# Block 0's scores spread by VectorE and turned once in fp32; first up weights and block 1's normalisation on GpSimd

## The reference

```
x = x + attention(layernorm(x), ctx)         # q, k, v projections, softmax over 120 keys
h = layernorm(x)
probs = softmax(h @ router.T)                # 8 experts
k = argmax(clip(gelu(h @ w1.T + b1) @ w2.T + b2)) + 1        # 1 to 6, for each token
score[e] = probs[e] if rank(e) < k else 0
x = x + sum_e score[e] * (silu(h @ gate[e].T) * (h @ up[e].T)) @ down[e].T     # 336 hidden units each
```

## Time and profile before

| | |
|---|---|
| median of 3 runs | 754.36 us (754.0 to 754.42) |
| the profiled execution, its own time | 754.58 us |
| its span, first to last instruction | 752.8 us |
| granted TensorE clock | 1.000 |
| PE busy | 741.4 us (98%) |
| DVE busy | 646.3 us (86%) |
| POOL busy | 578.4 us (77%) |
| ACT busy | 550.5 us (73%) |

### The profile page before, as it was taken

The page is one execution under the profiler, slowest core; times in us unless marked ns, Lnnn a source line. Parts: engine busy times, 40 slices in busy tenths (PEclk is TensorE's granted clock), DMA queues, the critical chain, the costliest instruction groups (busy, mean ns, idle before and its releaser), DMA issues.

```text
span 752.8 us, 13834 instructions
## 1 busy us (share of the span) xinstructions
PE 741.4 (98%) x3721; PEld 364.5 (48%) x3721; DVE 646.3 (86%) x1395; ACT 550.5 (73%) x978; POOL 578.4 (77%) x620
## 2 busy tenths in 40 slices
PE   8999999999999999999999999999999999999998
PEld 5544454444545445454544545445454544444445
DVE  7999888898878889888898988889888897978877
ACT  5997777777777776777767777776877767777664
POOL 2687977879796886968689696886968688696864
PEclk9999999999999999999999999999999999999999
DMA  9200211304033142322323133142322312120110
GB/s 351 71 15 15 64 36 36 78 14 85 16 76 78 28 100 50 76 54 60 78 40 87 38 78 74 27 98 48 77 54 61 80 28 56 28 57 15 28 30 29
DMA packets 107272, 45.40 MB, mean 60 GB/s; under 512 B 86873, under 2 KB 97113, under 8 KB 107225
## 3 DMA queue, kind: packets, MB, share of 16 engines
q1 hardware_dynamic: 106792, 44.39, 24.6%
q10 hardware_dynamic: 432, 0.48, 0.2%
HBM read 26.46 MB, written 10.78 MB: 49 GB/s over the span
## 4 chain that ended last, share of the span: by engine, by line
PE 80%; issue 6%; POOL 5%; DVE 5%; ACT 2%; DMA 0%; POOLq 0%; DVEq 0%; SPq 0%; ACTq 0%
PE bank L631 24%; PE bank L633 24%; PE bank L632 24%; POOL weighted L1204 3%; DVE bank L1558 2%; PE bank L514 2%; PE bank L541 1%; PE bank L627 1%; DVE hid_lo L1564 1%; PE bank L525 1%; PE bank L590 1%; PE bank L768 1%; PE bank L609 1%; POOL v_early L1146 0%; POOL apart L1172 0%
## 5 line engine op out<-in xcount | busy, mean ns | idle before, releaser
L1204 POOL TENSOR_TENSOR weighted<-silu,score_bc 128x512 f32<-128x512 f32 x336 | 432.2, 1302 | 118.9 <-ACT silu L969 114.8
L963 ACT ACTIVATE hid_hi<-bank 128x512 f16<-128x512 f32 x336 | 200.7, 597 | 169.4 <-DVE bank L1558 166.0
L1558 DVE SCALAR_TENSOR_TENSOR bank<-bank,h_scale,weighted 128x512 f32<-128x512 f32 x336 | 252.8, 752 | 70.4 <-PE bank L633 39.8
L969 ACT ACTIVATE silu<-bank,silu_scale 128x512 f32<-128x512 f32 x336 | 230.7, 687 | 14.8 <-PE bank L633 14.2
L1564 DVE TENSOR_TENSOR hid_lo<-bank,hid_hi 128x512 f16<-128x512 f32 x336 | 227.8, 678 | 3.1 <-ACT hid_hi L963 2.3
L631 PE MATMUL bank<-xn_lo,up_hi 128*128 128x512 f16 x336 | 127.6, 380 | 2.6 <-DVE hid_lo L1564 2.4
L631 PE MATMUL bank<-xn_lo,gate_hi 128*128 128x512 f16 x336 | 127.6, 380 | 1.3 <-ACT silu L969 1.3
L633 PE MATMUL bank<-xn_hi,up_hi 128*128 128x512 f16 x336 | 127.4, 379 | 0.0
L632 PE MATMUL bank<-xn_hi,up_lo 128*128 128x512 f16 x336 | 127.4, 379 | 0.0
L633 PE MATMUL bank<-xn_hi,gate_hi 128*128 128x512 f16 x336 | 127.4, 379 | 0.0
L632 PE MATMUL bank<-xn_hi,gate_lo 128*128 128x512 f16 x336 | 127.4, 379 | 0.0
(11 more groups left out here) (200 smaller groups left out, 800.0 us busy)
## 6 DMA issues: line engine op xcount, KB each, us to landing
x_in<-in_x SPq DMA_DIRECT2D x16, 256.0 KB, 2.8
y_kept<-y_sb SPq DMA_DIRECT2D x60, 64.0 KB, 2.6
y_tok<-y_kept SPq DMA_DIRECT2D x15, 256.0 KB, 2.8
out<-out_sb SPq DMA_DIRECT2D x15, 256.0 KB, 2.2
xt_in<-in_x_t SPq DMA_DIRECT2D x14, 256.0 KB, 2.7
row_bc<-row_kept SPq DMA_DIRECT2D x14, 256.0 KB, 3.5
ctx_in<-in_ctx_t SPq DMA_DIRECT2D x14, 240.0 KB, 2.7
p_kept<-y_sb SPq DMA_DIRECT2D x10, 256.0 KB, 2.0
```

Source lines behind the costliest of these rows:

```text
L963: af(hid_hi[j % HRING][:], up_bank[j % U_BANKS][:], ACT.Copy).then_inc(hid_hi_ready, 1)
L969: af(silu[j % RING][:], gate_bank[(par + j) % G_BANKS][:], ACT.Silu, scale=silu_scale[:])\
L1204: g.tensor_tensor(weighted[j % RING][:], silu[j % RING][:], score_bc[par][:], ALU.mult)\
L1558: v.scalar_tensor_tensor(up_bank[j % U_BANKS][:], up_bank[j % U_BANKS][:], h_scale[:], weighted[j % RING][:], ALU.mult, ALU.mult).then_inc ...
```

## The change

Block 0's scores: VectorE's one `first_scores` writes the masked probability of each token 16 times side by side (128 tokens x 4 batches x 128 columns, fp32, into `y_tok`, which is free then); TensorE turns the four 128 x 128 pieces in fp32 straight into the bank that `score_spread` reads, which now also multiplies by 256. The split, the copy, the product with ones and zeros and their constants (one 64 KB DMA on ScalarE's queue) are gone. Further: the first third of up's high half, `weight_high(1)`, moves from ScalarE to GpSimd; `norm1` of block 1 moves from ScalarE to GpSimd as two operations over 128 x 512; block 1's values are copied out of PSUM by ScalarE, and GpSimd adds the bias in place (`value_bias(1)`). On TensorE `keys(5)` now stands ahead of `gate(0, 0, 2)` and of the score transposes. The counts of `v_raw_ready` go up by one, since one more value copy is counted.

```diff
-            def score_transposes(n):
-                pe.wait_ge(s16_ready, n + 1)
+            def score_transposes():
+                pe.wait_ge(score_ready, 1)
                 pe.wait_ge(below_ready, 2)
                 for b in range(BB):
-                    last = transpose(x0[0:2 * EXPERTS, :].bitcast(F16)[:, b * P:(b + 1) * P], score16[:, b, :],
-                                     ident16_sb)
-                last.then_inc(st_done, 1)
-
-            def score_broadcast(n):
-                pe.wait_ge(st_ready, n + 1)
-                mm(x0[:], sel_sb, score_t[:], start=True, stop=True).then_inc(bc_done, 1)
+                    last = transpose(x0[:, b * P:(b + 1) * P], y_tok[:, b * P:(b + 1) * P], ident_sb)
+                last.then_inc(bc_done, 1)
...
-            gate(0, 0, 2)
-            score_transposes(0)
             pe.wait_ge(kmin_ready, 1)
             keys(5, 1, x1)
-            score_broadcast(0)
+            gate(0, 0, 2)
+            score_transposes()
             attend(1, y_bank)
...
-            def norm1(n, par, lo, hi):
-                act.wait_ge(ln1_shift, n + 1)
-                wait(act, t1_done, n)
-                for b in range(lo, hi):
-                    last = af(xn_nat[:, b, :], x_in[par][:, b, :], ACT.Identity, bias=shift1[:, b:b + 1],
-                              scale=rstd1[par][:, b:b + 1])
-                if hi == BB:
-                    last.then_inc(xn_ready, 1)
...
-            def score_copy(n):
-                act.wait_ge(st_done, n + 1)
-                wait(act, bc_done, n)
-                af(score_t[:], x0[0:2 * EXPERTS, :].bitcast(F16)[:, 0:NT], ACT.Copy).then_inc(st_ready, 1)
-
             def score_spread(n, par):
                 act.wait_ge(bc_done, n + 1)
                 wait(act, weighted_ready, TILES * (n - 1))
-                af(score_bc[par][:], x0[:], ACT.Copy).then_inc(bc_ready, 1)
+                af(score_bc[par][:], x0[:], ACT.Copy, scale=S_SCALE).then_inc(bc_ready, 1)
...
-            norm1(1, 1, 0, 2)
             exps(0)
-            norm1(1, 1, 2, BB)
+            values(1, y_bank)
             turned_probs(0)
...
             exps(1)
-            weight_high(1)
             router_exps(0)
             nc.scalar.preload_act_table(ACT.Silu)
             gated(0, 0, 0)
             turned_probs(1, up_bank[1])
             weight_high(2)
-            score_copy(0)
+            score_spread(0, 0)
             gated(0, 0, 1)
-            score_spread(0, 0)
             weight_sums(8)
...
-                else:
+                elif n == 0:
                     g.tensor_tensor(shift1[:], less1[:], rstd1[par][:], ALU.mult).then_inc(ln1_shift, 1)
+
+            def norm1(n, par):
+                pool.wait_ge(ln1_less, n + 1)
+                pool.wait_ge(ln1_rstd, n + 1)
+                pool.wait_ge(t1_done, n)
+                g.tensor_tensor(xn_nat[:], x_in[par][:], over(less1[:], P), ALU.add).then_inc(ln1_shift, 1)
+                pool.wait_ge(ln1_shift, n + 1)
+                g.tensor_tensor(xn_nat[:], xn_nat[:], over(rstd1[par][:], P), ALU.mult).then_inc(xn_ready, 1)
...
             rstd_1(0, 0)
             rstd_1(1, 1)
+            norm1(1, 1)
             pool.wait_ge(rest_in, 16)
+            value_bias(1)
             rstd_2(0)
             weight_high(0, 0, FIRST_TILES)
             x2_low(0, 0)
             weight_high(0, FIRST_TILES, PART)
+            weight_high(1, 0, PART)
             route_probs(0)
             rank_over(0)
-            pool.wait_ge(s16_ready, 1)
+            pool.wait_ge(score_ready, 1)
             rstd_1(2, 0)
             weigh(0, 0, 0)
...
+            def first_scores():
+                dve.wait_ge(over_ready, 1)
+                shape = [P, BB, EXPERTS, ROWS]
+                v.scalar_tensor_tensor(y_tok[:].rearrange("p (b e r) -> p b e r", b=BB, e=EXPERTS),
+                                       rank_less[:].unsqueeze(3).broadcast_to(shape), 0.0,
+                                       prob[:].unsqueeze(3).broadcast_to(shape), ALU.is_le, ALU.mult)\
+                    .then_inc(score_ready, 1)
...
@@ -1698,9 +1676,7 @@
             route_rank(0)
             aggregate_1_waits(2)
             aggregate_1(2)
-            scores(0)
-            split_scores(0)
-            values(1, y_bank)
+            first_scores()
             weight_low(1)
```

More of the change, by code:

```diff
@@ L86, with program @@
 SKIPPED, LAST_LAG, FIRST_STILL = (10, 16), 5, 15
-def program(nc, x, x_t, ctx_t, consts, consts16, gate_t, up_t, down_t, out):
+def program(nc, x, x_t, ctx_t, consts, gate_t, up_t, down_t, out):
     x_blocks = x.rearrange("(t p) (b d) -> t p b d", b=BB, p=P)
@@ L209, in program @@
         out_sb = [sb(f"out_sb{k}", [P, BB, P]) for k in range(2)]
-        consts_in, rest_in, consts16_in = sem("consts_in"), sem("rest_in"), sem("consts16_in")
+        consts_in, rest_in = sem("consts_in"), sem("rest_in")
         weights_in = [sem(f"weights_in{n}") for n in range(9)]
@@ L246, in program @@
                              "score_ready"))
-        s16hi_ready, s16_ready, st_done, st_ready, bc_done, bc_ready = (
-            sem(n) for n in ("s16hi_ready", "s16_ready", "st_done", "st_ready", "bc_done", "bc_ready"))
+        bc_done, bc_ready = sem("bc_done"), sem("bc_ready")
         spread_hi_ready, score_up_ready, spread_lo_ready, units_in, rows_ready = (
@@ L600, in probs_transposes @@
                 if isinstance(n, int) and n == 1:
-                    pe.wait_ge(v_raw_ready, 2)
+                    pe.wait_ge(v_raw_ready, 3)
                 for b in range(BB):
@@ L621, in keys @@
                 if is_ahead(n):
-                    pe.wait_ge(v_raw_ready, 4)
+                    pe.wait_ge(v_raw_ready, 5)
                 elif dst is x1 and not is_early(n):
@@ L674, in up @@
                 if isinstance(t, int) and t == 0 and j == 2:
-                    pe.wait_ge(v_raw_ready, 3)
+                    pe.wait_ge(v_raw_ready, 4)
                 wait(pe, hid_lo_ready, n - U_BANKS + 1)
@@ L772, in _ @@
             pe.wait_ge(rest_in, 16)
-            pe.wait_ge(consts16_in, 16)
             turn_first_x()
@@ L796, in _ @@
             probs_transposes(1, up_bank[1])
-            pe.wait_ge(v_raw_ready, 1)
+            pe.wait_ge(v_raw_ready, 2)
             values(4, 0, up_bank[2])
             gate(0, 0, 1)
-            gate(0, 0, 2)
-            score_transposes(0)
             pe.wait_ge(kmin_ready, 1)
             keys(5, 1, x1)
-            score_broadcast(0)
+            gate(0, 0, 2)
+            score_transposes()
             attend(1, y_bank)
@@ L1035, in _ @@
             act.dma_start(consts_sb[:, FIRST_CONSTS:], consts[:, FIRST_CONSTS:]).then_inc(rest_in, 16)
-            act.dma_start(consts16_sb[:], consts16).then_inc(consts16_in, 16)
             act.wait_ge(consts_in, 16)
@@ L1144, in value_bias @@
             def value_bias(n):
-                pool.wait_ge(v_raw_ready, n - 1)
+                pool.wait_ge(v_raw_ready, n)
                 g.tensor_tensor(v_early[n][:].rearrange("p (b d) -> p b d", b=BB),
@@ L1415, in values @@
                 dve.wait_ge(vp_done, n + 1)
-                if not isinstance(n, int) or n != 1:
-                    wait(dve, o_done, n)
+                wait(dve, o_done, n)
                 v.tensor_tensor(values_of(n)[:].rearrange("p (b d) -> p b d", b=BB),
@@ L1420, in values @@
                                 bv_sb[0:CTX, :].unsqueeze(1).broadcast_to([CTX, BB, P]), ALU.add)\
-                    .then_inc(v_early_ready if isinstance(n, int) and n == 1 else v_ready, 1)
+                    .then_inc(v_ready, 1)
             def residual(n, par, lo, hi, src=x0):
@@ L1504, in route_rank @@
                 v.tensor_reduce(rank[:], ahead[:], AX.X, ALU.add).then_inc(rank_ready, 1)
+            def first_scores():
[5 more added lines that the diff above has]
+                    .then_inc(score_ready, 1)
             def scores(n):
                 dve.wait_ge(over_ready, n + 1)
-                if isinstance(n, int) and n == 1:
-                    dve.wait_ge(s16_ready, 1)
-                else:
-                    wait(dve, spread_lo_ready, n - 1)
+                wait(dve, spread_lo_ready, n - 1)
                 v.scalar_tensor_tensor(score[:], rank_less[:], 0.0, prob[:], ALU.is_le, ALU.mult)\
                     .then_inc(score_ready, 1)
-            def split_scores(n):
-                dve.wait_ge(score_ready, n + 1)
-                v.tensor_scalar(score16[:, :, 0:EXPERTS], score[:], S_SCALE, None, ALU.mult).then_inc(s16hi_ready, 1)
-                dve.wait_ge(s16hi_ready, n + 1)
-                v.scalar_tensor_tensor(score16[:, :, EXPERTS:], score[:], S_SCALE, score16[:, :, 0:EXPERTS], ALU.mult,
-                                       ALU.subtract).then_inc(s16_ready, 1)
             def result_squares(n):
@@ L1721 @@
     down = np.asarray(L0_ffn_down_w).reshape(EXPERTS, P, TILES, ROWS).transpose(0, 3, 2, 1).reshape(P, TILES * P)
-    col = np.arange(P)
```

(3 more changed lines are left out.)

5 lines of the change are left out of this document (removed).

## The result

The changed kernel takes 755.95 us in the median of 14 runs (755.22 to 756.39), the kernel before 754.35 in the median of 14 (754.0 to 754.99). The ratio is 1.0020, with a 95% interval from 1.0013 to 1.0027: 1.6 us slower, from 1.0 to 2.0. The profiled execution took 756.23 us, its span is 754.3.

What follows compares the result with a forecast made beforehand. TensorE, full from 130 to 220 us, was taken to keep any lead-in lateness: 754.58 us profiled plus 0.65 for the late first hidden product gives 755.2, less 0.2 for the median 755.0; range 754.3 to 755.7, with the first rival 753.5 to 755.9.

Steps and rivals of the forecast that it cites:

- The signs that it named: Profile after: `weight_low` near 2.3 us, first silu near 28.8, scores ready near 30.9, first weigh right behind `row`, `score_bc` long there.
- TensorE is full further on, and what is late stays: From 130 to 220 us TensorE is busy 90.00 of 90.00 us; its lateness on entering stays to the end.
- Up's high half holds gate's `weight_low`: Lead-in: GpSimd's operation, taken as 1.9 us, makes VectorE's 640-column `weight_low` get going 1.40 us later.
- ScalarE gives back 0.25: Router's exponentials, freed of up's high half, start 0.05 after VectorE's step instead of 0.30, leaving the chain 1.15 us late.
- `first_scores` 0.75: VectorE's new scores operation in the lead-in takes 0.75 us, between ends of 0.43 and 1.14; scores ready at 30.90.
- The short way is hidden behind `rstd_1(2, 0)`: Before the first weigh: 1.05 us gained for `score_bc`, but GpSimd runs `rstd_1(2, 0)` first; weigh starts 0.7 after `score_bc`.
- `rstd_1(2, 0)` takes 1.92 us as before: GpSimd ahead of the first weigh: runs from 30.98 to 32.90, so the weigh starts at 32.95, 0.84 late.
- Normalisation and the constants' load are worth nothing: Lead-in: block 1's normalisation fits GpSimd's idle 6.94 us up to 17.52; the 64 KB load is off every wait found.
- The two don't hold each other: Rival at gate's `weight_low`: no stall, first hidden product 0.7 early, 753.65 us; chance 0.17.
- the lateness is hidden: Rival: later waits of TensorE inside the first turn take the lateness in, 754.4 us; chance 0.14.
- One more meeting, 1.05 us, slower: Rival, first turn: a `weight_low` or `ahead` finds a weigh begun before it, costing 1.05 us, 756.1; chance 0.11.

Runs made afterwards that it cites:

- e_scores_only: Kernel before with only the short way of the scores and TensorE's order; 754.45 us against 754.42 for the kernel before.
- e_up_only: Kernel before with only up's first high half moved from ScalarE to GpSimd; 755.69 us against 754.73 for the kernel before.
- e_up_back: Changed kernel with up's first high half back on ScalarE; 755.22 us against 754.73 for the kernel before.
- e_gap: Changed kernel with block 1's values added by VectorE again, between `first_scores` and `weight_low` of up; 755.17 us against 754.73 for the kernel before.
- e_gap_up_back: Changed kernel with block 1's values on VectorE again and up's first high half back on ScalarE; 754.64 us against 754.73 for the kernel before.
- e_rstd_free: Changed kernel without GpSimd's wait for the scores ahead of `rstd_1(2, 0)`; 756.01 us against 754.42 for the kernel before.
- e_rstd_later_only: Changed kernel with only `rstd_1(2, 0)` moved behind `rstd_2(1)` in the first turn, its wait for the scores removed; 756.58 us, +1.86 against the kernel before.
- e_sum_gap: Changed kernel with up's first high half back on ScalarE and VectorE's `row_sum(1)` ahead of `weight_low(1)`; 754.36 us against 754.42 for the kernel before.
- e_best: As e_sum_gap, with ScalarE making up's first high half behind block 1's turned probabilities; 753.84 us against 754.42 for the kernel before.

## Why the prediction came out as it did

The stated range was 753.5 to 755.9 and the median is 755.95, 0.05 above its upper end (for which the prediction has no working: its own terms reach 755.7). It also lies just above 755.87, from which the prediction would call the kernel slower, and to which it gave 0.11. The forecast of 755.0 had the sign and the first mechanism, and 0.65 us where 1.6 were measured. The signs that it named came, most of them near their number (`weight_low` 2.05 long for "near 2.3", the first silu at 28.88, the scores ready at 30.97, the weigh right behind `row` with `score_bc` long there).

- *TensorE is full further on, and what is late stays.* Right. From the first hidden product to the end of the span it is 719.2 us before, 719.3 after, and 718.9 to 719.5 in the kernels of the table, but for e_scores_only (720.1) and the two with `rstd_1` moved.
- *Up's high half holds gate's `weight_low`.* Right, with the size 1.17 us (2.05 - 0.88) instead of 1.40. GpSimd's operation took 1.67 and not 1.9: my rate came from the 640-column row. At the rate of the 1.67 that row would take 1.19 instead of 1.43; that the rest was itself a wait for VectorE, as the prediction had thought possible, fits but was not tested. e_up_only and e_up_back show the hold from both sides. The Trainium skill's rule (in "SBUF — State Buffer", section "Who interferes with whom": the instruction that issues first keeps the shared port to its end) agrees with the trace here on who waits, and nearly on how long: with 0.88 us of its own, VectorE's operation got going at 26.10, and GpSimd's ends at 26.29. One pair of rows does not follow it. In e_gap `weight_low` of up starts at 31.40, inside GpSimd's power operation (31.26, 1.01 long, two SBUF inputs), and takes its usual 1.14.
- *ScalarE gives back 0.25.* Right, 0.28.
- *`first_scores` 0.75.* 0.69.
- *The short way is hidden behind `rstd_1(2, 0)`.* Right; e_gap_up_back and e_scores_only show it.
- *`rstd_1(2, 0)` takes 1.92 us as before.* This is the step that failed: it took 2.71. I carried a length over from the old trace, though the change had taken away what stood beside it. Before, block 1's values, with one SBUF input, lay between scores and `weight_low` of up, and GpSimd's small additions ran beside them. With the values moved to GpSimd, where they are free, `weight_low` follows at 30.89 and has begun 0.16 us before `ve` comes at 31.05. I had the rule and counted its meeting at 24.9, but looked for meetings only where the change adds an operation, not where it takes one away. The price is 0.84 us on GpSimd (1.04 - 0.20); e_gap and e_rstd_free show it. It was partly made up for by luck: the terms before it were too large together, the scores being 0.95 late at their end where the sum had 1.26. With these at their measured size and 1.92 for `rstd_1(2, 0)` the forecast would have been 754.7, further off.
- *Normalisation and the constants' load are worth nothing.* Right for the normalisation; the load was tested only together with the short way, which is worth nothing with it gone (e_scores_only). Here VectorE's operations at 11.23 and 11.92, with at most one SBUF input, beside GpSimd's normalisation are 0.66 us each, as before.
- *Rivals.* "The two don't hold each other" is out, and so is "the lateness is hidden" (754.4). "One more meeting, 1.05 us, slower" is right in kind and size (0.84), but it sits in the lead-in, between `weight_low` and a four-column addition, not in the first turn.

With the two terms at their measured size the first hidden product is 1.06 us late, where 1.6 were measured for the whole, with 1.0 as the lower end. Up to 0.5 us have no cause that is shown. The two profiles are 1.5 apart, and 0.38 of it is the later start at gate's `weight_low`. That start is not a property of the changed kernel: e_rstd_free and e_rstd_later_only, with the same lists up to there, have 24.64 and 24.43. Measured the same way, start taken off, the time lies above what the first hidden product says by 0.7 us in e_rstd_free, 0.4 in e_sum_gap, 0.3 in e_up_back and e_scores_only, 0.2 in e_gap_up_back and e_best, 0.1 in e_up_only, and 0.2 below it in e_gap. The three largest (the changed kernel's own 0.5 among them), e_up_back and e_best are the kernels in which ScalarE copies block 1's values and GpSimd adds the bias; no run tests that move by itself. So I leave it open whether this is the spread of the runs (1.0 us within one kernel), that move, or something after the lead-in.

## What to carry to other kernels

Before moving an operation to an idle engine, look at what it holds while it runs, and who comes for that within its length. Look at what an operation kept apart, too: taking a harmless one out of a list lets its neighbours close up, and a hold between two engines can arise where nothing was added. And when a path gets shorter, read what else stands in the waiting engine's list ahead of the work that should profit.

## What the runs showed of the hardware that was not expected

- A four-column addition on GpSimd, 0.20 us alone, waits for the end of VectorE's wide operation: 1.04 us behind `weight_low` of up, 0.74 and 1.11 in e_rstd_free. GpSimd's power operation over four columns (1.01 us) did not get longer beside a `weight_low` that began after it, and did not hold it either (e_gap, 31.26 and 31.40).
- Such a wait shows only as the length of the waiting operation. No releaser is named for it.
- The 12 warm-up matmuls of 512 columns take 5.18 us in the kernel before, 5.30 in the changed one and 4.43 in e_up_only, whose lead-in is the same up to there. At 0.43 us apiece for 512 columns TensorE runs at 1.2 GHz, later in the same kernel at 0.22 apiece, at 2.4 GHz (the clock column of the profile says 1.00 in both, so it is the pace that shows it). The moment of the rise differs from one execution to the next, with the engine busy since 1.33 us in all of them. The first key product starts between 6.88 and 7.79 us in the twelve profiles, 7.79 in the changed kernel's. At gate's `weight_low` 0.5 us of it are left (24.43 to 24.93). So two single profiles of these kernels can't be set side by side closer than that without a common mark.

The warm-up matmuls and the first product behind them, on TensorE in order of time, one fence each for the kernel before, the changed one and e_up_only:

```profile
1.33 5.18 PE L768 MATMUL bank<-xn_hi 128*128 128x512 f16 x12 [1.33 <-POOL xn_hi L1087]
6.35 0.39 PE L499 MATMUL bank<-wq_even,consts_sb 128*128 128x128 f32 x2
```

```profile
1.33 5.30 PE L757 MATMUL bank<-xn_hi 128*128 128x512 f16 x12 [1.33 <-POOL xn_hi L1056]
6.42 0.64 PE L493 MATMUL bank<-wq_even,consts_sb 128*128 128x128 f32 x2
```

```profile
1.34 4.43 PE L768 MATMUL bank<-xn_hi 128*128 128x512 f16 x12 [1.34 <-POOL xn_hi L1086]
5.95 0.46 PE L499 MATMUL bank<-wq_even,consts_sb 128*128 128x128 f32 x2 [0.18 <-DVE wq_even L1654]
```
